# Two transformer layers on one core: new priorities for the order of the steps, and a second buffer for the MLP's float32 value

## The reference

```python
def layer0(x, y):                                # 16 heads of 16 features
    h = ln(x, ln1)
    q, k, v = rope(h @ sa_wq * scale), rope(h @ sa_wk), h @ sa_wv
    x = x + softmax_causal(q @ k.T) @ v @ sa_wo  # self-attention over 1024 tokens
    h = ln(x, ln2)
    q, k, v = rope(h @ ca_wq * scale), rope(y @ ca_wk), y @ ca_wv
    x = x + softmax(q @ k.T) @ v @ ca_wo         # attention to the 154 context tokens
    return x + gelu_tanh(ln(x, ln3) @ fc1 + b) @ fc2
def layer1(x, y):
    a = softmax_causal((x @ Wq) @ (y @ Wk).T / 4) @ (y @ Wv)
    h = ln(x + a, ln4)
    return gelu(h @ W1 + b1) @ W2 + b2 + h       # 256 -> 1024 -> 256
```

## Time and profile before

| | |
|---|---|
| median of 3 runs | 1098.04 us (1093.66 to 1100.06) |
| the profiled execution | 1102.32 us |
| its span | 1100.5 us |
| TensorE busy | 902.2 us (82%) |
| VectorE busy | 599.0 us (54%) |
| ScalarE busy | 481.1 us (44%) |
| GpSimd busy | 174.4 us (16%) |
| mean granted TensorE clock | 0.867 |

### The profile page before, as it was taken

How to read it: one execution, slowest core, us unless ns; L and a number is a source line. 1 busy time by engine, 2 the same in 40 slices (tenths; PEclk the granted TensorE clock), 3 DMA queues, 4 the chain that set the end, 5 groups by cost and what they waited for, 6 DMA issues and landing times.

```text
span 1100.5 us, 14705 instructions
## 1 busy us (share of the span) xinstructions
PE 902.2 (82%) x5504; PEld 484.9 (44%) x5504; DVE 599.0 (54%) x1355; ACT 481.1 (44%) x926; POOL 174.4 (16%) x139
## 2 busy tenths in 40 slices
PE   2577877699889889878969886999886898898788
PEld 1233334244744256333337433743322473562377
DVE  3664764776467753368555777765206703515530
ACT  1224342145356555443443443256764444453543
POOL 4332000001300022001013101300000030230143
PEclk9768878598889989979889986999998798897888
DMA  8875343400640224239023602324003145062052
GB/s 301 231 207 140 50 89 57 58 2 20 163 59 14 28 53 139 32 69 112 2 29 110 102 3 29 116 77 59 2 20 41 18 131 81 26 158 30 1 173 96
DMA packets 60010, 86.08 MB, mean 78 GB/s; under 512 B 14726, under 2 KB 45602, under 8 KB 59938
## 3 DMA queue, kind: packets, MB, share of 16 engines
q1 hardware_dynamic: 46372, 38.99, 22.4%
q10 hardware_dynamic: 13568, 46.14, 12.3%
HBM read 47.08 MB, written 10.49 MB: 52 GB/s over the span
## 4 chain that ended last, share of the span: by engine, by line
PE 52%; DVE 14%; DMA 10%; ACT 9%; issue 8%; SPq 5%; POOL 2%; ACTq 0%; POOLq 0%; DVEq 0%
PE ps_o L1043 10%; PE ps_chain L905 8%; PE ps_max L968 7%; ACT probs L1333 5%; PE ps_exp L925 5%; PE ps_exp L1001 5%; DVE mcol L1200 5%; SPq L763 4%; DMA QA<-part 3%; PE ps_chain L881 3%; PE ps_exp L929 2%; PE ps_chain L889 2%; DMA QC<-part 2%; DMA stage<-in_blocks 2%; DVE swap L1107 2%
## 5 line engine op out<-in xcount | busy, mean ns | idle before, releaser
L1333 ACT ACTIVATE probs<-ps_exp 128x512 f32<-128x512 f32 (+3 forms) x544 | 261.2, 522 | 248.5 <-PE ps_exp L1006 88.5
L1200 DVE TENSOR_REDUCE mcol<-ps_max 128x3 f32<-128x462 f32 (+5 forms) x496 | 290.5, 625 | 123.2 <-PE ps_max L970 65.6
L968 PE MATMUL ps_max<-KA,QA 96*128 96x512 bf16 (+3 forms) x384 | 118.3, 360 | 53.5 <-DVE mcol L1200 28.2
L1001 PE MATMUL ps_exp<-QA,KA 98*128 98x512 bf16 (+3 forms) x384 | 119.1, 346 | 31.4 <-ACT probs L1333 24.9
L1381 POOL TENSOR_TENSOR part<-rot,part 128x512 bf16<-128x512 f32 (+1 forms) x36 | 40.5, 1126 | 568.4 <-DVE part L1117 568.4
L905 PE MATMUL ps_chain<-hup,ring 128*128 128x512 f32 x384 | 113.2, 436 | 3.7 <-ACT gel L1287 2.5
L1398 POOL TENSOR_TENSOR hid<-gel,hid 128x512 fp32r<-128x512 f32 x64 | 83.8, 1309 | 142.9 <-ACT gel L1325 142.9
L1323 ACT ACTIVATE hid<-ps_chain,col 128x512 fp32r<-128x512 f32 x64 | 44.1, 689 | 121.5 <-PE ps_chain L905 121.3
L1001 PEld LDWEIGHTS ps_exp<-QA,KA 98*128 98x128 bf16 x384 | 36.1, 99 | 125.6 <-ACT probs L1333 100.9
L1043 PE MATMUL ps_o<-probs,V 128*17 128x512 f32 (+3 forms) x768 | 85.8, 521 | 3.6 <-ACT probs L1333 2.6
L968 PEld LDWEIGHTS ps_max<-KA,QA 96*128 96x128 bf16 x384 | 37.4, 104 | 114.3 <-DVE mcol L1200 69.9
(11 more groups left out here) (118 smaller groups left out, 1211.9 us busy)
## 6 DMA issues: line engine op xcount, KB each, us to landing
ring<-keep ACTq DMA_DIRECT2D x64, 512.0 KB, 3.3
QA<-part SPq DMA_DIRECT2D x72, 128.0 KB, 5.2
QC<-part SPq DMA_DIRECT2D x72, 128.0 KB, 5.2
keep<-ring ACTq DMA_DIRECT2D x8, 1024.0 KB, 5.3
KA<-part SPq DMA_DIRECT2D x48, 128.0 KB, 5.0
xb<-in_x SPq DMA_DIRECT2D x8, 512.0 KB, 6.2
stage<-in_blocks ACTq DMA_DIRECT2D x8, 512.0 KB, 8.6
out<-xb SPq DMA_DIRECT2D x4, 512.0 KB, 3.1
```

The costliest lines, as they stand in the source:

```text
L968: mm = pe.matmul(dst, q, kk, start=True, stop=not causal)
L1001: mm = pe.matmul(bank[:, q0:CH], KA[:, g // NT, hh, (g % NT) * P:(g % NT + 1) * P], QA[:, hh, q0:CH], start=True, stop=(r < 0))
L1200: dve.tensor_reduce(dst, src, AX.X, ALU.max).then_inc(s_max_done, 1)
L1333: act.activation(probs[:, n % 2, h, q0:CH], ps_exp[exp_nth[s] % 2][:, q0:CH], ACT.Exp).then_inc(s_exp_done, 1)
```

## The change

Three tables and two constants of `order()` get other values: `COST`, `LANDS`, `AHEAD`, `PRIORITY` with `CHUNK_PRIORITY`, and `SLACK`. None of it is computed on the chip; it makes another order of the same 1721 steps. And `gel` gets a second half, so that ScalarE waits only for GpSimd's last but one reading of it; which half a step writes is `low_nth[s] % 2`.

```diff
-    "stats": (("dve", 4.5),), "tr": (("pe", 0.6), ("act", 0.95)),
+    "stats": (("dve", 4.5),), "tr": (("pe", 0.55), ("act", 1.15)),
...
-PRIORITY = (6, 4, 1, 7, 8, 5, 3, 2, 0, 9, -3)
-CHUNK_PRIORITY = {0: (3, 4), 1: (3, 4), LAST: (1.5, -2)}
+PRIORITY = (31.6, 0.74, -16.76, 17.05, 60.2, 51.18, -5.48, -31.68, -72.98, 115.93, -38.66)
+CHUNK_PRIORITY = {0: (-24.15, 47.78), 1: (1.83, 7.47), LAST: (-4.77, -25.58)}
...
-        gel = sb("gel", [P, CH])
+        gel = sb("gel", [P, 2, CH])
...
-                        if low_nth[s] > 1:
-                            act.wait_ge(s_low, low_nth[s] - 1)
-                        dst = gel[:, :].rearrange("p (f n) -> p f n", f=KT)
+                        if low_nth[s] > 2:
+                            act.wait_ge(s_low, low_nth[s] - 2)
+                        dst = gel[:, low_nth[s] % 2, :].rearrange("p (f n) -> p f n", f=KT)
...
-                    act.wait_ge(s_low, low_nth[s] - 1)
-                    act.activation(gel[:, :], bank[:, :], gelu, bias=bias).then_inc(s_chain_free[u % 2], 1)
+                    act.wait_ge(s_low, low_nth[s] - 2)
+                    act.activation(gel[:, low_nth[s] % 2, :], bank[:, :], gelu, bias=bias).then_inc(s_chain_free[u % 2], 1)
...
-                    pool.tensor_tensor(hid[:, n % 2, 1, :], gel[:, :], hid[:, n % 2, 0, :],
+                    pool.tensor_tensor(hid[:, n % 2, 1, :], gel[:, low_nth[s] % 2, :], hid[:, n % 2, 0, :],
```

More of the change, by code:

```diff
@@ L198 @@
     "wload": (("act", 0.6),), "wsave": (("act", 0.6),), "wsplit": (("act", 1.1), ("pool", 2.4)), "fetch": (("act", 2.4),),
-    "stats": (("dve", 4.5),), "tr": (("pe", 0.6), ("act", 0.95)),
-    "proj": (("pe", 1.9), ("act", 0.6), ("dve", 4.0)), "place": (("dma", 3.8),),
+    "stats": (("dve", 4.5),), "tr": (("pe", 0.55), ("act", 1.15)),
+    "proj": (("pe", 1.8), ("act", 0.7), ("dve", 4.5)), "place": (("dma", 3.8),),
     "v": (("pe", 2.2), ("act", 0.55)), "wo": (("pe", 2.1), ("dve", 0.65)),
     "up": (("pe", 1.4), ("act", 1.4), ("pool", 1.3)), "down": (("pe", 1.41), ("act", 0.6)), "res": (("dve", 0.65),),
-    "max": (("pe", 0.3), ("dve", 0.62)), "row": (("pe", 0.15), ("dve", 0.6), ("dma", 1.3)),
-    "exp": (("pe", 0.25), ("act", 0.5)), "pv": (("pe", 1.0),), "evac": (("act", 0.5),),
-    "turn": (("pe", 0.5), ("dve", 0.6)), "addatt": (("dve", 0.65),), "lnout": (("dve", 2.4),),
+    "max": (("pe", 0.3), ("dve", 0.62)), "row": (("pe", 0.15), ("dve", 0.65), ("dma", 1.3)),
+    "exp": (("pe", 0.25), ("act", 0.56)), "pv": (("pe", 1.0),), "evac": (("act", 0.6),),
+    "turn": (("pe", 0.45), ("dve", 0.75)), "addatt": (("dve", 0.65),), "lnout": (("dve", 2.4),),
     "ctxk": (("pe", 1.3), ("act", 0.6), ("dve", 3.5), ("dma", 3.8)), "ctxv": (("pe", 2.6), ("act", 0.7)),
@@ L208 @@
 DMA_LATENCY = 2.2
-LANDS = {"wload": 4.0, "wsave": 5.0, "fetch": 4.0}
+LANDS = {"place": 1.3, "ctxk": 1.3, "row": -1.0, "wload": 4.0, "wsave": 5.0, "fetch": 4.0}
 LOW_LATER = 0.9
@@ L216 @@
 PRO, POST, CMAX, SMAX, SEXP, PV, TURN, POSTL, CMAXL, CTX, SPLIT = range(11)
-PRIORITY = (6, 4, 1, 7, 8, 5, 3, 2, 0, 9, -3)
-CHUNK_PRIORITY = {0: (3, 4), 1: (3, 4), LAST: (1.5, -2)}
-SLACK = (0.0, 0.0, 0.0, 0.0, 0.0, 0.0, 0.1, 0.1, 0.6, 0.0, 0.0)
-AHEAD = 4.0
+PRIORITY = (31.6, 0.74, -16.76, 17.05, 60.2, 51.18, -5.48, -31.68, -72.98, 115.93, -38.66)
+CHUNK_PRIORITY = {0: (-24.15, 47.78), 1: (1.83, 7.47), LAST: (-4.77, -25.58)}
+SLACK = (1.99, 0.18, 0.0, -0.01, 0.12, -0.43, 0.02, 0.3, 0.26, -0.29, 0.07)
+AHEAD = 7.45
 def cross_maxes(chunks):
@@ L560, in build @@
         maskf = rot[:, :, :].rearrange("p a b -> p (a b)")[:, 0:MASKW]
-        brow = gel[0:len(BIAS_ROWS), 0:E]
+        brow = gel[0:len(BIAS_ROWS), 0, 0:E]
         bpart = [QC[0:len(BIAS_ROWS), i, 0:E] for i in range(3)]
@@ L1392, in _ @@
                     half_of_input_free(pool, s)
-                    pool.tensor_tensor(hup[:, 1, :, cols], gel[:, :].rearrange("p (f n) -> p f n", f=KT),
+                    pool.tensor_tensor(hup[:, 1, :, cols], gel[:, low_nth[s] % 2, :].rearrange("p (f n) -> p f n", f=KT),
                                        hup[:, 0, :, cols], ALU.subtract).then_inc(s_low, 1)
```

## The result

The changed kernel takes 1126.74 us, median of 4 runs (1121.29 to 1128.33), beside 1096.01 us for the kernel before, measured with it (1093.66 to 1100.06). The ratio is 1.0268, with a 95% interval of 1.0217 to 1.0318: 31 us slower. The forecast was 1113 us, slower, in a range of 1082 to 1133. The direction and the range held, and 14 us of the size were missed.

The account below looks back on a forecast made before the run. TensorE was taken to bound the kernel, busy 902.2 of 1100.5 us. Terms 6.5 + 9 + 3 - 6 - 2 + 3 + 1 + 1 = +15.5 us on the 1098.0 median gave 1113 us, range 1082 to 1133.

Parts of the forecast that it names:

- First MLP and the projection behind it: Chunk 1's second-half qs projection, moved behind the first MLP, has less cover before its maxima: +6.5 us (0 to +9.2).
- Between chunk 1's MLPs: Nine more maxima on VectorE and fewer exponentials on TensorE in this stretch: +3 us (0 to +6.5).
- Projection qs of chunk 3, first half: Projection placed before ln3's second half, removing most of a 7.17 us TensorE wait: -6 us (-7.2 to -4).
- Normalizations of chunk 2: Less TensorE work between statistics and transposes of ln3 and ln2, against a 5.0 us chain: +3 us (0 to 6).
- The last MLP: Last normalization chain left in the open ahead of it, 13.6 us idle against 3.7: +9 us (+7 to +11).
- Exponentials in a row: More exponentials in runs, where with two banks the third waits for ScalarE: +1 us (0 to 10.5).
- table loads: ScalarE's function changes 15 times instead of 13, two more loads of 1.28 us: +1 us (0 to 2.6).
- The second buffer: Second half of gel removes ScalarE's waits to write gel elsewhere in the kernel: -2 us (0 to -8).
- Faster: Rival: TensorE's small waits for maxima and exponentials shrink by two fifths throughout, giving 1087 us; chance 0.28.
- No change: Rival: waits behind the first MLP and in chunk 1's stretch are absorbed, +2, 1100 us; chance 0.18.
- Clock: Rival: after long idle at the first and last MLPs, following steps run at low clock, +10 us, 1123; chance 0.08.

Follow-up runs that it names:

- swap_up02: Changed kernel with the steps from the end of chunk 1's second MLP through chunk 2's first MLP in the order of before: 1124.61 us, ratio 1.0249.
- cut_mlp01: Changed kernel with the order of before up to the end of chunk 1's first MLP, new order after it: 1124.52 us, ratio 1.0268.
- cut_mlp03: Changed kernel with the order of before up to the end of chunk 3's first MLP, only the end new: 1098.18 us, ratio 1.0020.
- before_again: The kernel before, unchanged, run once more for a second trace: 1094.75 us, ratio 0.9994.
- cut_mlp00: Changed kernel with the order of before up to the end of chunk 0's first MLP, new order after it: 1119.28 us, ratio 1.0224.
- fill_after: Changed kernel plus 113 unused matmuls on TensorE ahead of ten long waits, same order: 1116.36 us, ratio 1.0180.
- buffer_only: Kernel before with only the second half of gel added, old tables kept: 1082.74 us, ratio 0.9880.

## Why the prediction was right in direction and short in size

**The sum of the waits held, in part by luck.** +15.5 us were forecast as waits, +17.4 are in the trace as idle time of TensorE. But 8.8 of the 17.4 lie in the start, for which the sum has no term; the places that it does name come to 8.6 us, little more than half. Term by term, from the table of stretches:

- *First MLP and the projection behind it, +6.5:* idle 12.5 to 18.2, +5.7 behind the MLP, and 2.7 to 0 in it, for the wait at L929 is gone: +3.0 of idle time, less than half the term. Exchanging that place gives 5 us back in time, which the intervals don't tell from nothing. The releaser was wrong for most of it (VectorE's L1133 behind the rope, not the DMA): I had counted what stands between on TensorE and not what stands ahead on VectorE.
- *Between chunk 1's MLPs, +3:* idle +4.0, and 1.7 more in the MLP behind it. But the exchange of the stretch gives nothing, so this size is not shown by a run.
- *Projection qs of chunk 3, first half, -6:* idle 29.0 to 20.2, -8.8, a little beyond the bound of -7.2. The wait of 7.17 us at L1001 is gone. ScalarE writes gel there without a wait (a row with one would end in brackets), and the table load follows:
```profile
586.43 1.04 ACT L1287 ACTIVATE gel<-ps_chain,col 128x256 f32<-128x256 f32 x2
...
590.03 1.28 ACT L1323 ACT_TABLE_LOAD   x1
591.33 0.69 ACT L1323 ACTIVATE hid<-ps_chain,col 128x512 fp32r<-128x512 f32 x1
```
- *Normalizations of chunk 2, +3:* idle +3.8 and -1.6 in the two stretches; the exchange of the first (swap_up02) gives 2 us, which is within the noise. With the order of before up to chunk 1's first MLP (cut_mlp01) the waits of transposes for normalized tiles between there and chunk 3 are 11.1 us more than in cut_mlp03, beyond the bound of 6 that I gave for chunk 2; the longest of them, 4.16 us, lies between chunk 1's MLPs.
- *The last MLP, +9:* the chain itself idles 7.27 + 3.04 = 10.3 us against 3.7, +6.6 where I had 13.6 against 3.7; that is just under the lower bound. The last two stretches together idle 17.1 before and 25.1 after. The cut gives 15.5 us in time for the whole end, of which 8.9 are idle time and 5.8 slower matmuls.
- *Exponentials in a row +1, table loads +1:* ScalarE has two instructions more (928 against 926), the loads; neither can be told apart in the totals.
- *Not in the sum:* the start up to the first MLP, +8.8 us idle. I had not compared the two orders there. A wait of 6.06 us of TensorE at L968 stands in it, whose cause is on VectorE: L1114 waits 6.98 us at the head of its queue for a buffer that a DMA reads, and the maxima of attention stand behind it (before_again has such a wait of L1114 too, 5.77 us at 145.98, but TensorE's longest wait behind it there is 3.12 us):
```profile
139.39 0.32 DVE L1114 CAST part<-rot 128x308 bf16<-128x308 f32 x1 [6.98 <-DMA KA<-part]
...
141.24 0.50 PE L968 MATMUL ps_max<-KA,QA 96*128 96x384 bf16 x1 [6.06 <-DVE mcol L1200]
```
cut_mlp00 gives back 7 us by the medians for start and first MLP together.

**What failed: the clock, which I priced at nothing in the sum and at +10 us with a chance of 0.08 in the rival.** It was 15.1 us in the traces. I had looked at the two longest new waits and at three MLP steps behind each. The low level costs in every stretch with new waits: 19 us more of it behind the first MLP, 19 between chunk 1's MLPs, 16 ahead of chunk 2's first, 15 in the start, 10 in the last two; the other stretches and the MLPs have less of it than before, and the whole has 58 us more. fill_after shows that about 10 us of it hang on ten waits. The forecast with this term, 1113 + 15, is 1128. The Trainium skill ("TensorE: Matmul & The Clock Gate", Why this matters for your kernels), cited for that rival, asks for no idle gaps between bursts of matmuls. This case agrees, with 58 us more at the low level for 17 us more idle time.

**The second buffer, -2, bounds 0 and -8:** it is -14 us on the order of before (ratio 0.9880), outside the bounds, and -4 us on the new one. I had counted the waits that it removes. Those come to little in idle time, and the gain shows as 11 us less busy time of TensorE at a higher clock, of which all runs together bear out 8.5 at most. Which waits raised the clock in which stretch, the traces don't show, so the cause of this gain stays open: the largest fall is ahead of the last but one MLP, where idle time is the same (14.6 and 14.5 us) while the clock reads 0.85 in before_again and 0.94 in buffer_only:
```profile
963.20:1024.50 61.30, 46.78 (x314) 18.11 (x313) 29.23 (x78) 29.89 (x56) 5.71 (x5) 0.94 0.28 45
```
On the new order the buffer's error is small, -4 where -2 stood; the +15 of clock make the miss.

**The rivals.** *Faster* falls: the small waits are 67.5 us, not under 50. *No change* falls: the waits behind the first MLP and at the end were not absorbed. *Clock* was the right mechanism beside the sum, and its 10 us were nearer than the sum's nothing.

## What to carry to other kernels

In this kernel, which TensorE bounds, new idle time came with about as much again of slower matmuls: 1.9 times its length in the whole (32.5 us of span for 17.4 us idle), 2.2 and 1.7 times in the two cuts (30.6 for 13.9, 14.7 for 8.9). It is no fixed rate, since the second buffer changed the time at the same idle time. Compare mean granted clocks of the whole program before the waits one by one. When an order of steps changes, look at what stands ahead in VectorE's queue as well as at what TensorE has in between, and look at every stretch, the start too. An order that gives cover to one kind of chain (here the placing of projections) can take it from another (the normalizations). A second half for the small buffer between two engines was worth 14 us on one order and about 4 on the other, so measure such a buffer apart from an order that was changed with it.

## What the runs showed of the hardware

- TensorE's empty work pays here: 28 us of unused matmuls, put into ten waits (and 7 us longer than the idle time that they took away), took 18.6 us off the same useful matmuls and 10 us off the time.
- The upper clock level read 0.95 through one execution of before and 1.00 in the next of the same kernel, with MLP steps 2.82 us apart in both. Mean clocks of two traces can be compared only after a look at the clock inside an MLP without idle time; the times of matmuls there show whether the clock or only its reading differs.
- A change of ScalarE's function is the load alone in the trace after: the load ahead of chunk 1's first MLP starts at 590.03, takes 1.28 us, and the next instruction starts at 591.33. The Trainium skill ("ScalarE: Activation LUTs", What ACT_TABLE_LOAD costs) adds a drain of about 1380 ns to it. That is not to be seen there: the instruction ahead ends at 590.02.
